# Left and right products stored token by token instead of feature by feature

## The reference

```
x  = layernorm(pair) * ln1_w + ln1_b
left  = sigmoid(x @ left1)  * (x @ left2)
right = sigmoid(x @ right1) * (x @ right2)
p[s, k, e] = sum over r of left[s, r, e] * right[k, r, e]      (for every feature e)
q  = (layernorm(p) * ln2_w + ln2_b) @ out_w * sigmoid(x @ gate)
x1 = pair + q
then, on x1: left = x1 @ (W_left + W_eq) + biases; right_sum = sum over one axis of (x1 @ W_right + b)
out = layernorm((left * right_sum * sigmoid(x1 @ W_gate + b)) @ W_out + b_out + x1) * scale + bias
```

## Time and profile before

| what | value |
|---|---|
| median of three runs | 113.8 us |
| profiled execution, first to last instruction (span) | 112.1 us |
| TensorE (PE) busy | 92.5 us, 83% |
| VectorE (DVE) busy | 77.3 us, 69% |
| ScalarE (ACT) busy | 66.6 us, 59% |
| GpSimd (POOL) busy | 62.6 us, 56% |
| mean granted TensorE clock | 0.976 of full speed |

### The profile page before, as it was taken

The page is one execution under the profiler, slowest core; times in us unless marked ns, Lnnn a source line. Parts: engine busy times, 40 slices in busy tenths (PEclk is TensorE's granted clock), DMA queues, the critical chain, the costliest instruction groups (busy, mean ns, idle before and its releaser), DMA issues. The chain is left out here.

```text
span 112.1 us, 1886 instructions
## 1 busy us (share of the span) xinstructions
PE 92.5 (83%) x600; PEld 72.3 (64%) x600; DVE 77.3 (69%) x284; ACT 66.6 (59%) x110; POOL 62.6 (56%) x78
## 2 busy tenths in 40 slices
PE   1997599789999899999979999999999996495000
PEld 1994368567776799545445789878877994394000
DVE  1528697986769800599975869699979963996500
ACT  0614888687785166795499463993797399330000
POOL 5037974599950040025488585587865492699400
PEclk9999999999999999999999999999999999999955
DMA  3669997000000000000000000000023006029996
GB/s 60 126 111 171 146 146 75 0 0 0 0 0 9 0 0 0 0 0 3 0 0 0 3 6 0 0 0 6 0 35 59 0 0 94 0 34 144 147 144 100
DMA packets 33486, 4.54 MB, mean 40 GB/s; under 512 B 33348, under 2 KB 33476, under 8 KB 33476
## 3 DMA queue, kind: packets, MB, share of 16 engines
q1 hardware_dynamic: 31632, 4.00, 27.6%
q10 hardware_dynamic: 1844, 0.41, 1.8%
HBM read 2.31 MB, written 2.10 MB: 39 GB/s over the span
## 5 line engine op out<-in xcount | busy, mean ns | idle before, releaser
L596 DVE TENSOR_TENSOR lr<-bank,sig_lr 128x512 f32<-128x512 f32 x16 | 15.9, 1044 | 3.7 <-ACT sig_lr L431 3.7
L817 PE MATMUL bank<-lr_blk,xnT 64*128 64x256 f32 x128 | 16.5, 392 | 1.0 <-ACT xnT L421 0.7
L352 POOL TENSOR_TENSOR t_tok<-p_sb,rstd 128x512 f32<-128x512 f32 x7 | 10.2, 1462 | 11.8 <-DVE rstd L666 11.8
L360 POOL TENSOR_TENSOR x_low<-x1T,x_high 128x512 fp32r<-128x512 f32 x8 | 10.3, 1290 | 7.5 <-ACT x_high L501 7.5
L817 PEld LDWEIGHTS bank<-lr_blk,xnT 64*128 64x128 f32 x128 | 11.8, 186 | 4.0 <-issue 2.3
L660 DVE BATCH_NORM_STATS2 stats<-p_sb 128x6 f32<-128x64 f32 x64 | 8.5, 211 | 7.0 <-ACT p_sb L465 7.0
L368 POOL TENSOR_TENSOR oT<-o_a,rsum 128x512 f32<-128x512 f32 x8 | 8.7, 1089 | 6.4 <-DVE o_a L706 4.2
L431 ACT ACTIVATE sig_lr<-bank 128x512 f32<-128x512 f32 x16 | 9.6, 598 | 3.9 <-PE bank L817 3.9
L581 DVE BATCH_NORM_STATS2 stats<-x_tok 128x6 f32<-128x64 f32 x64 | 8.9, 213 | 3.5 <-DMA x_tok<-in_x 3.3
L978 PEld LDWEIGHTS bank<-wout_blk,oT 128*128 128x128 f32 x64 | 8.1, 191 | 4.0 <-POOL oT L368 3.2
L978 PE MATMUL bank<-wout_blk,oT 128*128 128x128 f32 x64 | 8.8, 281 | 2.2 <-POOL oT L368 2.2
(11 more groups left out here) (104 smaller groups left out, 199.8 us busy)
## 6 DMA issues: line engine op xcount, KB each, us to landing
x_tok<-in_x SPq DMA_DIRECT2D x14, 128.0 KB, 4.2
out<-sq SPq DMA_DIRECT2D x7, 256.0 KB, 3.4
x_tok<-in_x SPq DMA_DIRECT2D x3, 64.0 KB, 2.7
w_rep<-in_weights ACTq DMA_DIRECT2D x1, 180.5 KB
out<-sq ACTq DMA_DIRECT2D x1, 128.0 KB, 3.7
out<-sq SPq DMA_DIRECT2D x1, 128.0 KB, 3.8
x_tok<-in_x ACTq DMA_DIRECT2D x1, 64.0 KB, 2.7
row_rep<-in_rows ACTq DMA_DIRECT2D x1, 32.0 KB, 5.1
```

Source lines behind the costliest of these rows:

```text
L352: nc.gpsimd.tensor_tensor(place(t_tok[:, c % 2], 0, SPC), even_first(p_sb[:, :, s]), even_first(rstd[:, 1:2, s]).to_broadcast([P, 2, SPC / ...
L360: nc.gpsimd.tensor_tensor(x1_low[:, c % 2], x1T[:, c % 3], x1_high[:, c % 2], ALU.subtract).then_inc(x1_low_ready, 1)
L596: nc.vector.tensor_tensor(lr[:, :, s].rearrange("p f s -> p s f"), src[:, :, 2 * CH:4 * CH], sig_lr[:, j % 3].rearrange("p (s f) -> p s f" ...
L817: last = nc.tensor.matmul(dst, xnT[half, c, k * P:(k + 1) * P], lr_blk[half].rearrange("p g m c -> p g (m c)"), start=True, stop=True, ski ...
```

## The change

`lr` becomes [128 partitions, 128 tokens, 64 features]. L596 writes the eight tokens of a half as one contiguous run of 512 elements. L871 reads 128 elements of a feature with a step of 64 elements (256 bytes), for the stationary and for the moving operand. `y` and `yn` stay the same two contiguous halves of the memory. No instruction is added or removed, and no wait is changed.

```diff
-        lr = sb("lr", [P, 2 * CH, P])
+        lr = sb("lr", [P, P, 2 * CH])
...
-        y = lr[:, 0:CH, :].rearrange("p f s -> p (f s)").rearrange("p (s c) -> p s c", c=CH)
-        yn = lr[:, CH:2 * CH, :].rearrange("p f s -> p (f s)").rearrange("p (s c) -> p s c", c=CH)
+        y = lr[:, 0:P // 2, :].rearrange("p s f -> p (s f)").rearrange("p (s c) -> p s c", c=CH)
+        yn = lr[:, P // 2:P, :].rearrange("p s f -> p (s f)").rearrange("p (s c) -> p s c", c=CH)
...
-                nc.vector.tensor_tensor(lr[:, :, s].rearrange("p f s -> p s f"), src[:, :, 2 * CH:4 * CH],
+                nc.vector.tensor_tensor(lr[:, s, :], src[:, :, 2 * CH:4 * CH],
...
-                last = nc.tensor.matmul(bank[:, e // 4, (e % 4) * P:(e % 4 + 1) * P], lr[:, e, :], lr[:, CH + e, :],
+                last = nc.tensor.matmul(bank[:, e // 4, (e % 4) * P:(e % 4 + 1) * P], lr[:, :, e], lr[:, :, CH + e],
```

## The result

The changed kernel takes 120.22 us (median of four runs, 119.81 to 120.30) against 113.94 for the kernel before on the same chip: ratio 1.0535, 95% interval 1.0475 to 1.0595. It is slower by 6.3 us; the forecast was 120.2 us. The profiled execution has a span of 118.4 us.

What follows compares the result with a forecast made beforehand. TensorE was taken to bound L871's stage, uncovered, with the writer mostly covered. Span 112.1 - 0.7 + 7.0 = 118.5 us, plus 1.7 to the median: 120.2 us; range 112.9 to 127, own case 117 to 123.

Steps and rivals of the forecast that it cites:

- The writer's price: L596 on DVE: 684 ns instead of 1044 once its output is contiguous, 0.36 us less for each of 16.
- Where it counts: End of the projections: last half starts 0.30 us earlier, last multiply is 0.36 us shorter; earlier savings are covered.
- No cover for the reader: L871's stage, 37.8 to 45.3 us: TensorE alone works, so each nanosecond added to a record lands on the kernel's end.
- The reader's price: L871 on TensorE: a record takes 223 ns, 110 more, so 64 records add 7.0 us.
- The prediction's other sum: L871: 0.70 ns per element added to the present pace, 5.7 us more over the stage.
- Why 223: L871: memory gives one stepped element per 1.74 ns, as for DVE's L673 and L596; 128 of them take 223 ns.
- TensorE does not notice: Rival for L871: records keep 113 ns, only the writer's gain is left, 113.1 us; chance 0.21.
- The two operands disturb each other: Rival for L871: both stepping streams collide, say 335 ns a record, 127 us, range 123 to 130; chance 0.13.
- Two readings per record: Rival for L871: a float32 record reads its columns twice, 446 ns, 21.3 us more, 134.4 us; chance 0.12.
- The short step of 24 words at 2.50 ns: Skill's DVE figure applied to L871: 320 ns a record and 13 us more; no row shows such a step.
- The clock: L871's stage: the prediction fails if the granted clock, 1.00, falls while TensorE waits for its operands.
- The range: Whole kernel: 117 to 123 us for the forecast case; from no step price, 112.9, into the disturbed case, 127: 0.81.

Runs made afterwards that it cites:

- e3: Kernel before, L596 walking in pairs of neighbouring tokens, features outside, lr layout and reader unchanged: 113.23 us against 113.92, ratio 0.9926.
- e1: Changed kernel with only the writer's half: L596 writes token by token, L871 reads side by side; 113.24 us against 113.92 for the kernel before, ratio 0.9936.
- e6: Kernel before, only the moving operand of fp32r products L937, L938 and L940 stepping by 16 elements: 120.34 us (one run).
- e8: Kernel before, only the 32 transposes L895 reading x_tok with a step of 32 elements: 114.17 against 113.97 us, one run each.
- e4: Changed kernel with another step of L871's stationary and moving operands in each of 8 banks: 117.87 us (one run).
- e5: Changed kernel, L871's stationary operand side by side, moving operand in another pattern of runs or lone elements per bank: 117.72 us (one run).
- e2: Kernel before with only the reader's half: L596 writes feature by feature, L871 reads with a step of 64 elements; 120.70 us, ratio 1.0584.
- e7: Kernel before, L596 walking in runs of 8 tokens per feature, both sources stepping for each element: 113.86 against 113.88 us, ratio 0.9997.

## Why the prediction was right

- *The writer's price.* Taken: 684 ns from L724, 0.36 us less. Measured: 682. Right, and for the reason given; e3 adds that pairs in the output are enough.
- *Where it counts.* Forecast were 0.30 + 0.36 = 0.66 us at the end of the projections, nothing elsewhere. Shown: 0.67 in the changed kernel, 0.68 in e1, with nothing gained in the earlier part.
- *No cover for the reader.* Each added nanosecond was to land on the end; 6.80 us in the stage and none lost or won in the 67 us behind it.
- *The reader's price.* Forecast were 223 ns between records, 7.0 us; measured 217 and 6.8. The prediction's other sum, 0.70 ns added to the present pace, gives 202 ns, and is further off.
- *Why 223.* Here the step was right in size and wrong in kind. I took 1.74 ns for a lone element from DVE and let each record read once. The runs speak for two readings of 0.85 ns in its place (inferred, see e6 and e8). I had both halves among the rows: that fp32r's pace of 0.47 ns, halved, "would still be 0.94 ns, close to the 0.88 it uses now" as an argument for no cost, and that a record may read twice as an argument for 446 ns. Put together they give 2 x 0.94 x 128 = 241 ns. A memory that gives one lone element per 1.74 ns is ruled out: the fp32r records of e6 and the transposes of e8 get them at 0.85 ns. So nothing in the runs ties TensorE's price to DVE's, and that the number taken from DVE came within 3% was luck.
- *The rivals.* "TensorE does not notice" was the right account of transposes and the wrong one of this line. "The two operands disturb each other" fell with the 220 ns of one operand alone in e4. "Two readings per record" was right in its name, not in its price of 446 ns. The short step of 24 words at 2.50 ns that the Trainium skill gives for DVE ("Vector Engine (DVE) Microarchitecture Reference", Measured stream behaviour on trn2) has no counterpart on TensorE here: no step of e4 or e5 cost more than 236 ns a record, 1.84 ns an element, though 24 itself was not run.
- *The clock.* The prediction named a fall of the clock as a way to fail. It fell, and did not matter: the records stood 216 to 218 ns apart at either level.
- *The range.* The prediction gives two, 117 to 123 us as this case's own and 112.9 to 127 us with a chance of 0.81. The 120.22 us lie in both.

## What to carry to other kernels

Ask of every operand how many of the elements that it takes one after the other share 16 bytes, and hold the price against the pace that the record has anyway: here a lone element was free for a transpose, doubled a float32 matmul of 128 columns, and cost an elementwise instruction of DVE half again. A layout trade between a covered writer and an uncovered reader is decided by the reader, however much larger the saving looks in busy time (5.8 us against 0.68 that counted). Before moving data around, try another walk over the same layout: pairs were enough for both sides.

## What the runs showed of the hardware

- TensorE's granted clock fell in the middle of the slowed stage, though records followed each other without a gap. By stretch, TensorE alone, after:

```profile
37.40:40.00 2.60, 2.60 (x12) 0.97 0.00 0
40.00:43.00 3.00, 3.00 (x16) 0.50 0.00 0
43.00:46.00 3.00, 3.00 (x16) 0.96 0.00 0
46.00:49.00 3.00, 3.00 (x15) 1.00 0.00 0
```

  From 40 to 43 us it was at 0.50, the 1.2 GHz level, and before and after at 2.4 GHz. Ahead of the fall lay 0.21 us of idle time and records held up by their operands. The distance between the records was 216 to 218 ns at either level, so this stage lost nothing by it: it waits for its operands, not for the array. In the kernel before, the same stage ran at 1.00 throughout. The clock fell at the same place in e2 (0.51 from 40 to 43 us), but not in e4 and e5, whose stages begin with banks at 111 to 118 ns a record and then hold records of up to 236 ns: 1.00 from 37.4 to 52 us. What makes it fall is not shown.
- A LDWEIGHTS of 128 columns has a longer record where it steps (310 against 192 ns in L871, 189 against 141 in the transposes), which in the second case is no loss. Durations of single records do not tell the price; distances between their starts do.
- DVE takes two sources that alternate between two rows at full speed (687 ns in e3 against 682 with everything side by side), and not sources that go round eight rows (1036 ns in e7).
